# Low halves of the mean layer's input moved from GpSimd to VectorE, tile loop reordered

## What is computed

```python
x = _layernorm(x + L0(x, adj, weight))                    # binary layer
x = _layernorm(x + L1(x, adj, ...))                       # attention layer
#   L1: sigmoid(attn_a * (attn @ (x @ W_sa)) + attn_b * (adj @ (x @ W_gcnb) + b_gcnb))
x = _layernorm(x + L2(x, adj, W, b))                      # mean layer
#   L2: A = (adj != 0);  deg = sum(A, axis=0);  A @ (x @ W + b) / deg[:, None]
x = _layernorm(x + L3(x, adj, W_stack))                   # two GAT layers
```

## Time and profile before

| what | value |
|---|---|
| median of three runs | 474.75 us |
| profiled execution, its own time | 473.92 us |
| its span, first to last instruction | 472.1 us |
| TensorE matmul busy | 461.1 us (98%) |
| VectorE busy | 373.5 us (79%) |
| ScalarE busy | 230.7 us (49%) |
| GpSimd busy | 189.8 us (40%) |
| mean granted TensorE clock | 0.997 |

### The profile page before, as it was taken

One profiled execution on the slowest core, in us unless ns is written; L12 is line 12 of the kernel. 1 busy time (PEld: TensorE's weight loads), 2 busy tenths in 40 slices (PEclk: granted clock), 3 DMA queues, 4 the chain that ended last, 5 costly groups with the idle time before them and its releaser, 6 DMA issues.

```text
span 472.1 us, 5613 instructions
## 1 busy us (share of the span) xinstructions
PE 461.1 (98%) x1838; PEld 302.4 (64%) x1838; DVE 373.5 (79%) x832; ACT 230.7 (49%) x407; POOL 189.8 (40%) x186
## 2 busy tenths in 40 slices
PE   8999999999999999999999999999999999999993
PEld 6999745545555588877544444554557546778882
DVE  5688799999998689848137746999955697899984
ACT  5979529991888543333434532442333475342200
POOL 1444675631435136954001541453440073456641
PEclk9999999999999999999999999999999999999998
DMA  8856310001358100000000000000000000000001
GB/s 295 281 174 194 122 42 0 1 1 59 117 180 198 41 1 1 0 1 1 1 0 0 0 1 1 1 0 1 0 1 0 1 1 1 0 20 15 22 24 40
DMA packets 16500, 21.73 MB, mean 46 GB/s; under 512 B 9328, under 2 KB 13060, under 8 KB 16472
## 3 DMA queue, kind: packets, MB, share of 16 engines
q1 hardware_dynamic: 15464, 20.06, 13.8%
q0 software_dynamic: 464, 0.79, 0.8%
q10 hardware_dynamic: 544, 0.52, 0.3%
HBM read 19.99 MB, written 1.39 MB: 45 GB/s over the span
## 4 chain that ended last, share of the span: by engine, by line
PE 76%; DVE 16%; issue 3%; DMA 2%; SPq 1%; POOL 1%; ACT 0%; POOLq 0%; DVEq 0%
PE psum L1580 16%; PE psum L1423 11%; PE psum L1384 11%; PE psum L1680 8%; PE psum L1617 6%; PE psum L1365 6%; PE psum L1474 4%; PE psum L1560 3%; DVE ST L1075 3%; PE psum L1286 2%; PE psum L1532 2%; PE psum L1446 2%; PE psum L1651 2%; DVE rm L1024 2%; DMA adj_rows<-in_adj_dram 2%
## 5 line engine op out<-in xcount | busy, mean ns | idle before, releaser
L1580 PE MATMUL psum<-QT,xT 128*128 128x512 f32 (+3 forms) x264 | 108.0, 542 | 0.0
L460 POOL TENSOR_TENSOR es<-es,ST 128x512 f32<-128x512 f32 (+3 forms) x60 | 76.0, 1267 | 55.1 <-ACT ST L646 53.4
L641 ACT ACTIVATE ST<-psum 128x512 f32<-128x512 f32 (+3 forms) x66 | 36.1, 547 | 91.7 <-DVE rm L1024 81.9
L1580 PEld LDWEIGHTS psum<-QT,xT 128*128 128x128 f32 (+1 forms) x264 | 48.2, 186 | 42.5 <-issue 35.9
L1024 DVE TENSOR_TENSOR rm<-psum,rm 128x512 f32<-128x512 f32 (+3 forms) x60 | 37.4, 624 | 40.6 <-PE psum L1580 40.4
L1680 PE MATMUL psum<-Wh,ST 128*128 128x256 f32 (+3 forms) x242 | 55.1, 380 | 0.0
L1617 PE MATMUL psum<-ST,Wh 128*128 128x512 f32 (+3 forms) x132 | 54.4, 543 | 0.6 <-DVE ST L1075 0.6
L387 POOL TENSOR_TENSOR rstd<-veps,nhalf 128x1 f32<-128x1 f32 (+1 forms) x44 | 29.2, 664 | 62.9 <-DVE veps L778 62.7
L415 POOL TENSOR_TENSOR esumb<-esumb,eb 128x1354 f32<-128x1354 f32 (+1 forms) x10 | 34.5, 3452 | 46.3 <-ACT eb L548 46.3
L1423 PE MATMUL psum<-eb,x_all 128*128 128x512 f32 (+3 forms) x132 | 51.9, 542 | 0.0
L1384 PE MATMUL psum<-adjT,x_all 128*128 128x512 f32 (+3 forms) x132 | 50.1, 542 | 0.0
(11 more groups left out here) (177 smaller groups left out, 775.0 us busy)
## 6 DMA issues: line engine op xcount, KB each, us to landing
adj_rows<-in_adj_dram SPq DMA_DIRECT2D x10, 677.0 KB, 4.9
rows<-in_adj_dram SPq DMA_DIRECT2D x10, 677.0 KB, 4.0
x_all<-in_x_dram SPq DMA_DIRECT2D x5, 256.0 KB, 4.0
out_dram<-xs SPq DMA_DIRECT2D x10, 128.0 KB, 1.7
W<-in_L_gnn_W_stack_dram SPq DMA_DIRECT2D x2, 512.0 KB, 6.1
W3B<-in_L_gnn_W_stack_dram SPq DMA_DIRECT2D x8, 128.0 KB, 3.7
adj_rows<-in_adj_dram SPq DMA_DIRECT2D x1, 338.5 KB
rows<-in_adj_dram SPq DMA_DIRECT2D x1, 338.5 KB
```

The costliest lines, as they stand in the source:

```text
L460: nc.gpsimd.tensor_tensor(es[0:r, g % 2, 0:w], es[0:r, g % 2, 0:w], buf(g)[0:r, j, 0:w], ALU.add)\
L1580: last = nc.tensor.matmul(psum[0:r, SB[n % 3], 0:w], xT[l][:, k, j * P:j * P + r], QT[:, k, c0:c1], start=(k == 0), stop=(k == KD - 1))
```

## The change

GpSimd's `low_half` is removed and a function of the same name is added on VectorE, with the same operands and waits. VectorE's loop turn becomes `norm_apply(i)`, `attn_sum(i + 2)`, `attn_out(i + 1)`, `low_half(i)`, `mean_mask(i + 2)`. The first two low halves stand before the reciprocals of the degrees and before `mean_mask(3)`. GpSimd's queue is left with `rsqrt(i)` and, from the eighth on, `add_bias2(i - 7)`; the last seven bias sums follow the loop.

```diff
-            def low_half(i):
-                r = kk(i)
-                pool.wait_ge(xh_ready.sem, i + 1)
-                nc.gpsimd.tensor_tensor(xhl[0:r, i, 1, :], x_all[0:r, i, :], xhl[0:r, i, 0, :], ALU.subtract)\
-                    .then_inc(xl_ready.sem, 1)
+            LAG = 7
...
-            rsqrt(NB, 0)
-            rsqrt(NB, 1)
-            low_half(0)
-            low_half(1)
-            rsqrt(NB, 2)
-            low_half(2)
-            rsqrt(NB, 3)
-            for i in range(3, T):
-                if i + 1 < T:
-                    rsqrt(NB, i + 1)
-                low_half(i)
-                if i >= 4:
-                    add_bias2(i - 4)
-            for i in range(T - 4, T):
+            for i in range(T):
+                rsqrt(NB, i)
+                if i >= LAG:
+                    add_bias2(i - LAG)
+            for i in range(T - LAG, T):
                 add_bias2(i)
...
+            def low_half(i):
+                r = kk(i)
+                dve.wait_ge(xh_ready.sem, i + 1)
+                nc.vector.tensor_tensor(xhl[0:r, i, 1, :], x_all[0:r, i, :], xhl[0:r, i, 0, :], ALU.subtract)\
+                    .then_inc(xl_ready.sem, 1)
+
             attn_sum(0)
             scale_xb(3, 6)
             attn_out(0)
@@ -968,6 +961,7 @@
             norm_apply(NB, 0, vbuf[:, 0, :])
             attn_sum(2)
             attn_out(1)
+            low_half(0)
             dve.wait_ge(deg_ready.sem, 2 * T)
...
             norm_apply(NB, 1, vbuf[:, 1, :])
             attn_sum(3)
+            attn_out(2)
+            low_half(1)
             mean_mask(3)
-            attn_out(2)
-            attn_sum(4)
-            norm_apply(NB, 2, vbuf[:, 2, :])
-            mean_mask(4)
-            attn_out(3)
-            attn_sum(5)
-            mean_mask(5)
-            for i in range(3, T):
+            for i in range(2, T):
+                norm_apply(NB, i, vbuf[0:kk(i), i % 4, :])
+                if i + 2 < T:
+                    attn_sum(i + 2)
                 if i + 1 < T:
                     attn_out(i + 1)
-                norm_apply(NB, i, vbuf[0:kk(i), i % 4, :])
-                if i + 3 < T:
-                    attn_sum(i + 3)
-                if i + 3 < T:
-                    mean_mask(i + 3)
+                low_half(i)
+                if i + 2 < T:
+                    mean_mask(i + 2)
```

## The result

The changed kernel takes 481.56 us (median of 4 runs, 481.08 to 482.25) against 474.75: ratio 1.0142, interval 1.0129 to 1.0155. The forecast was 475.9 with a range of 474.3 to 477.0. The profiled execution took 481.08 us with a span of 479.3, 7.2 us more than before on both counts.

The account below looks back on a forecast made before the run. TensorE, busy in 98% of the span, was taken as the bound. Three waits of 1.44 us less 0.31 won make tile 10 1.1 us later: 475.9 us from a 474.75 median, range 474.3 to 477.0.

Parts of the forecast that it names:

- The gain at tile 3: TensorE at tile 3 of the mean layer's aggregation: its wait for GpSimd's low half goes, 0.31 us won.
- The price of the low half: VectorE's tile loop: each added low half costs 0.35 us, upper end 0.43.
- The root held by the mask: VectorE's tile loop: each root comes 0.03 us after the mask's end, adding 0.15 us per turn, 3.20 instead of 3.05.
- The rival of a root held by both operations: Tile loop: root 0.41 us after low half and mask, turn 3.59, total 479.0 us; chance 0.09 shared with starved last tile.
- the bias sum's collision from tile 7 on: Tile loop from tile 7: the bias sum meets norm_apply, which takes 0.82 instead of 0.41 us, 0.41 more per turn.
- 0.82 us for `norm_apply(10)`: Last tile: norm_apply meets one bias sum; high half 10 comes at 203.26, wanted at 202.92, 0.34 us late.
- 1.51 to a rival: Last norm_apply loses twice, waiting for two bias sums: 0.69 us more, 476.6 us in all; chance 0.17.
- the case of all seven sums: Last norm_apply waits for all seven bias sums: 4.5 us more; a starved last tile shared the chance of 0.09.
- Both rows: Earlier trace: norm_apply at 199.06 took 1.51 us; a mask-like operation at 66.19 beside a GpSimd queue took only 0.94.
- slower: Whole kernel: a time above 475.7 us, the line of 0.2%; chance 0.53, against 0.43 for same.
- 1.44 us of waits forecast at three tiles: TensorE waits for late high halves at tiles 8, 9 and 10: 0.67, 0.43 and 0.34 us; chance 0.43.

Follow-up runs that it names:

- e1: Changed kernel with GpSimd waiting for the attention layer's last norm_apply before its last eight bias sums: 474.64 us, 0.9993 of the kernel before.
- e2: Changed kernel with GpSimd's wait for the last norm_apply placed one bias sum later, after the first of the last eight: 474.42 us, one run.
- e12: Changed kernel without bias sums in the tile loop: six after waiting for the last norm_apply, five behind mean-layer roots; 474.16 us, 0.9990 of the kernel before.
- e14: Changed kernel with GpSimd waiting for the last norm_apply before its last sums, plus a one-input float32 VectorE operation ahead of low half 10: 474.07 us.
- e15: Changed kernel with four memsets ahead of the last norm_apply and GpSimd waiting for its own last root before the eight sums: 474.37 us.
- e7: Kernel before the change with bias sums seven tiles behind instead of four, nothing else: 474.80 us, ratio 0.9994.
- e8: Kernel before the change with only the low halves moved to VectorE, old loop order, sums four tiles behind: 477.79 us.
- e4: Changed kernel with 20 unused 512-column matmuls keeping TensorE busy while it waits for tile 10: 478.68 us, ratio 1.0077.
- e3: Changed kernel with bias sums four tiles behind instead of seven: 478.50 us.
- e5: Changed kernel with the last norm_apply alone written as an operation with two SBUF inputs: 482.51 us.
- e9: Changed kernel with four chained VectorE memsets between the wait for the last root and the last norm_apply: 481.81 us.
- e10: Changed kernel with two chained VectorE memsets between the wait for the last root and the last norm_apply: 483.27 us.
- e11: Changed kernel with one GpSimd memset between the last root and the first of the eight bias sums: 483.45 us.
- e13: Changed kernel with the last norm_apply in two-input form and three chained memsets ahead of it: 481.95 us.
- e16: Changed kernel in which each of the last six bias sums waits for the one ahead of it on GpSimd: 475.48 us.
- e6: Changed kernel with the bias sums replaced by one-input GpSimd operations, x not added to the bias rows: 475.38 us.

## Why the prediction was wrong

*Right.* The gain at tile 3 (0.31 us). The price of the low half (0.41 us, the next operation 0.33 to 0.35 later). The root held by the mask: 1.06 us in each of tiles 2 to 9, and the turn 3.19 us (timeline, as the earlier trace rows):

```profile
177.96 0.42 DVE L953 TENSOR_TENSOR xhl<-x_all,xhl 128x256 fp32r<-128x256 f32 x1
178.12 1.07 POOL L387 TENSOR_TENSOR rstd<-veps,nhalf 128x1 f32<-128x1 f32 x1 [2.13 <-DVE veps L765]
178.29 0.86 DVE L870 TENSOR_SCALAR maskT<-adjT 128x1354 fp32r<-128x1354 f32 x1
179.23 0.41 DVE L770 TENSOR_SCALAR x_all<-vbuf,mv,rstd 128x256 f32<-128x256 f32 x1
```

`norm_apply(7)` came at 191.98 for 191.95. The rival of a root held by both operations didn't happen, although the Trainium skill, page "SBUF — State Buffer", section "Who interferes with whom", read strictly, allows it; the trace disagrees with that reading: the root ends 0.04 us after the mask (179.19 against 179.15), not 0.41. The prediction also counts two VectorE operations with two inputs behind `veps`; only the low half has two, the mask has one.

*Mis-sized, small.* I took 0.41 us per turn for the bias sum's collision from tile 7 on. The rows show 0.26 (0.67 instead of 0.41): the sum is recorded from 0.47 us before `norm_apply` and not from 0.06 before it. So tiles 8 and 9 were late by 0.23 and 0.28 us instead of 0.67 and 0.43. Tile 10 was wanted a little later than the text had it, too: (202.28 - 192.25) / 4 is 2.51 us per tile, not 2.47.

*The step that failed* is the last tile. The text took 0.82 us for `norm_apply(10)`, gave 1.51 to a rival, and set aside the case of all seven sums ("4.5 us more"), because the earlier trace rows spoke against it; it shared a chance of 0.09 and lay outside the range. That case is what happened: 4.91 us, 4.5 over 0.41. Both rows were read without asking what broke GpSimd's queue. This is how GpSimd and VectorE go on around in the kernel before (timeline):

```profile
197.53 0.40 DVE L783 TENSOR_SCALAR x_all<-vbuf,mv,rstd 128x256 f32<-128x256 f32 x1
197.63 0.89 POOL L427 TENSOR_TENSOR bias<-bias,x_all 128x256 f32<-128x256 f32 x1
...
198.49 0.54 POOL L387 TENSOR_TENSOR rstd<-veps,nhalf 74x1 f32<-74x1 f32 x1
...
201.10 0.74 POOL L421 TENSOR_TENSOR xhl<-x_all,xhl 74x256 fp32r<-74x256 f32 x1 [0.68 <-ACT xhl L589]
```

At 199.06 two operations passed because the third waited for a semaphore (the 0.68 us), not because VectorE won the second or third turn. The 0.82 of the earlier trace rows had such a pause behind it as well: GpSimd's next operation came at 173.96, after 1.38 us of waiting. The earlier trace rows is the end of a run of eleven operations with which VectorE had taken turns from the start, its next operation always standing ready, 0.60 us each where the same form took 0.42 at 55.98 (timeline):

```profile
61.16 6.23 POOL L407 TENSOR_SCALAR xp<-x_all 128x256 f32<-128x256 f32 x11
...
62.34 0.60 DVE L807 CUSTOM_DVE_ANT_0 dots<-x_all,ubc 128x256 f32<-128x256 f32 x1
```

Single VectorE operations got in after one sum where the queue of sums began after a pause (e1, e2, e12, e14, e15); at the last tile of the changed kernel the root goes over into the sums without one. The text had listed what GpSimd does behind the last root, but it never asked what the removed low halves did for VectorE: low half 10 waited for the `norm_apply` and thereby broke the queue (e7 against e8).

That "slower" had the larger chance is mostly luck. Of the 1.44 us of waits forecast at three tiles, tiles 8 and 9 gave 0.51, and the loss that made the result came by another way.

*Missing from the sum* is the clock. The text followed a late tile through to the end one to one. Waits of up to 0.3 us cost only themselves, the one of 4.4 us also cost 2.6 us at half clock by the timeline (1.9 in tile 10, 0.7 in the projection) and 2.9 by the medians (e4).

## What to carry over

When an operation is moved off an engine, ask what its waits did for others: a wait in GpSimd's queue may be the only gap through which VectorE gets in. A run of GpSimd operations that follows a root without a pause, beside a VectorE operation on the path, is to be priced at its whole length; one wait of GpSimd for its own last result, or better for the VectorE result that matters, takes that price away (e15, e1). A wait that leaves TensorE idle for microseconds is to be priced with the clock that follows.

## What the runs showed of the hardware

Whether VectorE gets in between GpSimd's operations depends here on GpSimd's pauses. Ten times an operation of VectorE that met a GpSimd queue running unbroken since the last root was passed by everything up to the next pause: four sums 2.86 us (e3), five 3.64 (e8), seven 4.41 to 5.05 (e4, e5, e9, e10, e11, e13 and the changed kernel), two 1.51 (e16). The kernel before (1.51) and e7 (1.52) show it with a low half and a sum. It didn't matter whether it had one or two inputs, or whether it came 0.06 or 0.56 us after the first sum. With a pause of GpSimd's alone ahead of the queue the same operation got in after one sum (e15).

The Trainium skill, page "SBUF — State Buffer", section "Who interferes with whom", says that the one issued first holds the shared pair for its whole instruction; it says nothing of what follows it. In e11 the `norm_apply` was issued 0.08 us ahead of the first sum, while GpSimd's memset ran, and was passed by that sum too, so order of issue didn't decide there. No run here shows why a pause changes the order.

A pause ahead of a queue doesn't keep it open for good. In the kernel before, GpSimd's low half at 196.95 came after a pause of some 0.1 us (the root ahead of it ended at 196.82) and `norm_apply(9)` got in at 197.53 without delay; GpSimd went on without a pause through a sum and the root at 198.49, and `norm_apply(10)` was passed by two operations. In every case of being passed a root stood without a pause ahead of the queue, or, in e11, a root and a memset. Whether a long queue without a root in it can shut out an operation that arrives late wasn't tried; the eleven operations from 61.16 on didn't, but there VectorE always had its next operation ready.

TensorE's granted clock went from full to half around an idle time of 4.1 us (4.4 for its weight load) and was back some 7 us later in the changed kernel and e9, some 10 us later in e5, e10, e11 and e13, after idle times of 4.1 to 4.3 us in all of them. Shorter idle times went both ways: 2.1 us (e3), after a shorter wait before it, brought it down, 2.2 us (e8) and 1.3 us (e6) did not. So these runs give a price for such a wait, not a limit below which it is free.
